# Last batch of the last expert layer: five places for the sorted tokens, two weight loads between the scatters, the residual behind the normalization

## What is computed

```python
def _moe_mlp(x, gate_w, gate_b, w1, w2):
    logits = xf @ gate_w + gate_b
    one_hot = jax.nn.one_hot(jnp.argmax(logits, axis=-1), E, dtype=xf.dtype)   # E = 8
    h = jax.nn.gelu(jnp.einsum('td,edh->teh', xf, w1), approximate=True)       # 128 -> 512
    y = jnp.einsum('teh,ehd->ted', h, w2)                                      # 512 -> 128
    return jnp.einsum('te,ted->td', one_hot, y)

x = x + _msa(_layernorm(x, ln1_w, ln1_b), w_qkv, w_proj)
x = x + _moe_mlp(_layernorm(x, ln2_w, ln2_b), gate_w, gate_b, w1, w2)
```

## Time and profile before

| | |
|---|---|
| median of 3 runs | 2741.87 us (2741.44 to 2743.07) |
| the profiled execution | 2746.61 us |
| its span, first to last instruction | 2744.8 us |
| mean granted TensorE clock | 0.951 of full |
| busy share of the span: TensorE, VectorE, ScalarE, GpSimd | 85%, 68%, 65%, 34% |

### The profile page before, as it was taken

One profiled execution on the slowest core, in us unless ns is written; L12 is line 12 of the kernel. 1 busy time (PEld: TensorE's weight loads), 2 busy tenths in 40 slices (PEclk: granted clock), 3 DMA queues, 4 the chain that ended last, 5 costly groups with the idle time before them and its releaser, 6 DMA issues. The chain is left out here.

```text
span 2744.8 us, 44545 instructions
## 1 busy us (share of the span) xinstructions
PE 2339.9 (85%) x15879; PEld 907.7 (33%) x15958; DVE 1856.2 (68%) x3041; ACT 1775.1 (65%) x3759; POOL 938.8 (34%) x1573
## 2 busy tenths in 40 slices
PE   5789889888888999888889989978989988989934
PEld 3222223222322344444444444312223323423414
DVE  6779897878787575454555655678986787687410
ACT  4278777767766655545556556568877777777721
POOL 5450132453264266337415133014023222213222
PEclk8699999999999999999999999999999999999967
DMA  4331113112313312431322222112013213202304
GB/s 157 118 119 28 32 31 112 42 58 84 105 28 94 97 52 66 134 94 41 113 77 65 64 61 65 39 55 67 23 32 109 88 30 115 88 20 68 98 27 159
DMA packets 151965, 202.80 MB, mean 74 GB/s; under 512 B 23472, under 2 KB 104240, under 8 KB 151568
## 3 DMA queue, kind: packets, MB, share of 16 engines
q1 hardware_dynamic: 133344, 138.83, 16.8%
q0 software_dynamic: 17536, 59.58, 6.9%
q10 hardware_dynamic: 864, 1.53, 0.2%
HBM read 138.40 MB, written 57.93 MB: 72 GB/s over the span
## 5 line engine op out<-in xcount | busy, mean ns | idle before, releaser
L1240 ACT ACTIVATE PB<-bank 128x512 f32<-128x512 f32 (+3 forms) x2944 | 1440.1, 557 | 592.4 <-PE bank L946 308.2
L1420 DVE TENSOR_REDUCE small<-unit 128x1 f32<-128x1024 f32 x1024 | 1211.1, 1218 | 245.3 <-PE unit L966 235.5
L966 PE MATMUL unit<-RK 61*128 61x512 bf16 (+4 forms) x2764 | 871.9, 375 | 144.9 <-DVE small L1420 87.4
L1086 PE MATMUL bank<-PB,VP 128*32 128x512 f32 (+3 forms) x5888 | 760.8, 569 | 14.6 <-ACT PB L1240 7.9
L946 PE MATMUL bank<-RK 64*128 64x512 bf16 x2048 | 677.9, 387 | 72.8 <-ACT PB L1240 38.4
L1417 DVE CUSTOM_DVE_ANT_0 unit<-unit,maskb 128x640 f32<-128x640 f32 (+7 forms) x512 | 387.8, 770 | 325.3 <-PE unit L966 306.3
L966 PEld LDWEIGHTS unit<-RK 61*128 61x128 bf16 (+1 forms) x2816 | 211.6, 95 | 579.9 <-issue 254.2
L946 PEld LDWEIGHTS bank<-RK 64*128 64x128 bf16 x2048 | 154.4, 94 | 504.8 <-ACT PB L1240 327.5
L1655 POOL CAST small<-small 128x8 bf16<-128x8 f32 x192 | 36.7, 191 | 764.1 <-DVE small L1420 557.2
L942 PE MATMUL bank<-RK 128*128 128x512 bf16 (+2 forms) x959 | 279.0, 300 | 2.4 <-ACT PB L1240 0.9
L941 PE MATMUL bank<-RK 128*128 128x256 bf16 (+3 forms) x934 | 268.9, 299 | 12.4 <-ACT PB L1240 4.5
(11 more groups left out here) (183 smaller groups left out, 2044.1 us busy)
## 6 DMA issues: line engine op xcount, KB each, us to landing
RK<-q_parts SPq DMA_DIRECT2D x128, 96.0 KB
RK<-k_parts SPq DMA_DIRECT2D x128, 96.0 KB
RK<-rq_parts SPq DMA_DIRECT2D x48, 192.0 KB
RK<-rk_parts SPq DMA_DIRECT2D x48, 192.0 KB
q_parts<-SC SPq DMA_DIRECT2D x32, 256.0 KB, 2.8
k_parts<-SC SPq DMA_DIRECT2D x32, 256.0 KB, 2.8
XSB<-x_sorted SPq DMA_DIRECT2D x40, 192.0 KB, 4.1
y_sorted<-XSB SPq DMA_DIRECT2D x40, 192.0 KB, 2.1
```

Source lines behind the costliest of these rows:

```text
L966: p = e.matmul(unit[k // 2 - 2][:, c0:c1], slot(L, u, 0, 0, rows)[:, 128 * qt:128 * qt + 128], slot(L, u, 1, 0, rows)[:, c0:c1], start=Tru ...
L1086: p = e.matmul(bank[k][32 * j:32 * j + 32, c0:512], VP[:, 8 * (pr // 8) + kt, 9 * h:9 * h + 32], prob(L, t)[:, c0:512], start=(kt == 0), s ...
L1240: e.activation(prob(L, t)[:, c0:512], bank[k][:, c0:512], ACT.Exp, scale=LAYERS[L].scale).then_inc(bank_free[k], 1)
L1420: e.tensor_reduce(m, unit[k // 2 - 2][:, :], AX.X, ALU.max, negate=True).then_inc(bank_free[k], 1)
```

## The change

Three things, all for the last batch of the last layer:

1. The five groups of sorted tokens have a place each: three in `XSB` and two in `PB`, the buffer of the attention's exponentials, which is no longer in use. All five `xload` are written behind the last scatter, and none behind a `ystore`.
2. The `wload` of tile 0 is issued behind the second scatter DMA and that of tile 1 behind the sixth; the other thirteen stay behind the last scatter.
3. `residual` also waits for VectorE's `ln_out`.

```diff
@@ def dispatch
         for i in range(4):
             yield t - 0.5
             P.do("scatter", M, b, i, total=P.count(("scatter", b), 32), after=t)
+            if (M, b) == (1, B - 1) and i % 2 == 0:
+                load_weights(M, b, i // 2, mo["tile"], t)
+
+    def load_weights(M, b, j, first, t):
+
+        k = j if (M, b) == (1, B - 1) and j >= WXN else (first + j) % WXN
+        return P.do("wload", M, b, j, slot=k, total=P.count(("wload", k), 16), after=t)
@@ def experts
-                k = (first // GROUP + q) % XS
+                k = (first // GROUP + q) % XS if q < XS or not last else q
@@
-                k = j if last and j >= WXN else (first + j) % WXN
-                here["w", j] = P.do("wload", M, b, j, slot=k, total=P.count(("wload", k), 16), after=t)
+                here["w", j] = P.end["wload", M, b, j] if last and j < 2 else load_weights(M, b, j, first, t)
@@
-                xload(j // GROUP + 2, t)
+                if not last:
+                    xload(j // GROUP + 2, t)
@@
-        xload(0, P.end["scatter", M, b, 3])
-        xload(1, P.end["scatter", M, b, 3])
+        for q in range(EGROUPS if last else 2):
+            xload(q, P.end["scatter", M, b, 3])
@@ def build
+        def tokens(k):
+
+            return XSB[:, k, :] if k < XS else PB[:, k - XS, 0:128 * GROUP]
@@ gpsimd, residual
+                    if b == B - 1:
+                        g.wait_ge(ln_done, ln_no["g1", b, 1])
                     e.tensor_tensor(xs, xs, zs, ALU.add).then_inc(residual, 1)
@@ sync, xload
-                    if s.n > XS:
+                    if s.n > XS and k < XS:
                         g.wait_ge(ystored[k], ystores[s.n - 1 - XS].more["total"])
```

More of the change, by code:

```diff
@@ L419, in collect @@
         for i in range(4):
-            t1 = P.do("collect", M, b, i, total=P.count(("collect", b), 32), stored=[P.total["ystore", k] for k in range(XS)],
+            t1 = P.do("collect", M, b, i, total=P.count(("collect", b), 32), stored=[P.total.get(("ystore", k), 0) for k in range(EGROUPS)],
                       after=t)
@@ L745, in build @@
         collected = [sem("collected%d" % b) for b in range(B)]
-        ystored = [sem("ystored%d" % k) for k in range(XS)]
-        xloaded = [sem("xloaded%d" % k) for k in range(XS)]
+        ystored = [sem("ystored%d" % k) for k in range(EGROUPS)]
+        xloaded = [sem("xloaded%d" % k) for k in range(EGROUPS)]
         wloaded = [sem("wloaded%d" % k) for k in range(ETILES)]
@@ L1128, in tensor @@
                     for j in range(GROUP):
-                        p = e.transpose(bank[k][:, 128 * j:128 * j + 128], XSB[:, x["slot"], 128 * j:128 * j + 128], identf[:, :])
+                        p = e.transpose(bank[k][:, 128 * j:128 * j + 128], tokens(x["slot"])[:, 128 * j:128 * j + 128], identf[:, :])
                     p.then_inc(bank_full[k], 1)
@@ L1536, in vector @@
                     x, w = step_of["xload", M, b, j // GROUP].more["slot"], step_of["wload", M, b, j]
-                    o = XSB[:, x, 128 * (j % GROUP):128 * (j % GROUP) + 128]
+                    o = tokens(x)[:, 128 * (j % GROUP):128 * (j % GROUP) + 128]
                     g.wait_ge(bank_full[k], n)
@@ L1697, in gpsimd @@
                     g.wait_ge(*tail)
-                    for k in range(XS):
+                    for k in range(EGROUPS):
                         g.wait_ge(ystored[k], s.more["stored"][k])
@@ L1743, in sync @@
                     g.wait_ge(scattered[b], 128 * (M + 1))
-                    if s.n > XS:
+                    if s.n > XS and k < XS:
                         g.wait_ge(ystored[k], ystores[s.n - 1 - XS].more["total"])
-                    e.dma_start(XSB[:, k, :].rearrange("p (j d) -> p j d", d=128),
+                    e.dma_start(tokens(k).rearrange("p (j d) -> p j d", d=128),
                                 XSD[b][r:r + 128 * GROUP, :].rearrange("(j p) d -> p j d", p=128)).then_inc(xloaded[k], 16)
@@ L1753, in sync @@
                     e.dma_start(YSD[b][r:r + 128 * GROUP, :].rearrange("(j p) d -> p j d", p=128),
-                                XSB[:, k, :].rearrange("p (j d) -> p j d", d=128)).then_inc(ystored[k], 16)
+                                tokens(k).rearrange("p (j d) -> p j d", d=128)).then_inc(ystored[k], 16)
                 elif kind == "fetch":
```

## The result

| | before | after |
|---|---|---|
| median of 20 runs each, first comparison | 2744.38 us (2740.11 to 2756.64) | 2735.49 us (2723.93 to 2744.16) |
| ratio, 95% interval | | 0.9963, 0.9951 to 0.9974 |
| median, second comparison (11 and 6 runs) | 2746.57 us | 2734.22 us |
| ratio, 95% interval | | 0.9950, 0.9936 to 0.9964 |
| span of the profiled execution | 2744.8 us | 2731.3 us |

The changed kernel is faster by 8.9 us of the medians in the first comparison, 12.4 in the second. The predicted time, 2729.6 us, missed the first median by 5.9 us and the range by 1.9 us. The sum of 12.3 us is 0.45% of the time; the interval of the ratio, 0.26% to 0.49%, holds it.

The account below looks back on a forecast made before the run. The prediction took the last batch's serial chain to bound the end: normalization, GpSimd's scatters, then TensorE waiting for late token loads. Terms of -2.13, +2.51, -13.04 and +0.4 us took 2741.9 to 2729.6 us; 8-in-10 range 2726.8 to 2733.6.

Parts of the forecast that it names:

- The sum of 12.3 us: Last batch to the end: all terms together, -2.13 + 2.51 - 13.04 + 0.4 = -12.3 us.
- The two large terms: Last batch: residual after the normalization, -2.13 us; all five token loads at once, no TensorE waits between groups, -13.04 us.
- the price of an issue: GpSimd's queue between scatters: 1.26 us per issue, so two weight loads delay the last scatter by 2.51 us.
- The clock term: First expert group on TensorE: the clock may rise later, 5.3 us instead of 3.4; half of +0.85 us taken, +0.4.
- Part 2: Two weight loads between the scatters: last scatter 2.51 us later, nothing given back on TensorE.
- slow scatter: Last scatter's landing: early weights in the shared DMA queue could delay it by up to +1.7 us; 0 taken.
- The upper bound: Second early weight load: 6.4 us to landing, so the last scatter could land 1.7 us later.
- My lower bound: Early weight load: through after some 3.7 us, before the last scatter would land anyway, so 0 cost.
- The slow opening: Rival, last batch: scatters wait for early weights, five loads crowd the first, +1.7 us each; 2733.0 us, chance 0.18.
- The third load waiting for the weights: Rival, token loads: the third lands only when the weight stream is through; sum -4.1, 2737.8 us, chance 0.07.
- The first load: Rival, token loads: the first waits for the weight stream; sum +5.4 us, 2747.3 us, chance 0.03.

Follow-up runs that it names:

- e1: Changed kernel without the two early weight loads, all fifteen behind the last scatter; ratio to the kernel before 0.9944.
- e2: Kernel before with only the residual's wait for the normalization; ratio to the kernel before 0.9978.
- e5: Kernel before with five token places, each later token load issued as late as before but ahead of the store; one run, 2749.60 us, before 2742.66.
- e9: Changed kernel without early weight loads, third to fifth token loads issued only once the third tile's weights landed; ratio to the kernel before 0.9965.
- e12: Changed kernel with 82 additional TensorE products ahead of the last batch's first token turning; ratio to the kernel before 0.9944.
- slowed comparison: Changed kernel and two versions with 64 additional products, compared with the kernel before; all runs took 2,804 to 2,829 us, ratios 0.9999, 0.9998 and 1.0002.
- e4: Kernel before with only the two early weight loads between the scatters; ratio to the kernel before 0.9996.
- e6: Kernel before with five token places, three token loads at once, the last two behind the stores of groups 0 and 1; one run, 2756.16 us, before 2742.66.
- e3: Kernel before with only the five places and five token loads at once; ratio to the kernel before 0.9945.
- e13: Changed kernel without early weight loads, third to fifth token loads behind the third tile's weights, 74 additional TensorE products; ratio to the kernel before 0.9965.
- e10: Changed kernel with 64 additional TensorE products ahead of the last batch's first token turning; ratio to the kernel before 0.9951.
- e11: Changed kernel without early weight loads, third to fifth token loads behind the third tile's weights, 64 additional TensorE products; ratio to the kernel before 0.9953.
- e7: Same kernel as e11, run in the slowed comparison; ratio to the kernel before 1.0002.

## Why the prediction was wrong in its number and right in its mechanism

**The sum.** -12.3 us were forecast, the stretch gave -12.29. By pieces of the chain, each measured in both kernels:

| piece | forecast | measured |
|---|---|---|
| start of the stretch to the list of tokens for the last scatter (`IX`): 24.86, then 22.75 us | -2.13 | -2.11 |
| to the last scatter's landing: 12.03, then 14.66 | +2.51 | +2.63 |
| to the first `up` product of group 1: 13.33, then 13.02 | +0.4 | -0.31 |
| to the first `up` product of group 4: 30.16, then 17.13 | -13.04 | -13.03 |
| to the end: 25.67, then 26.20 | 0 | +0.53 |

The two large terms and the price of an issue were right. That the sum is right to 0.01 us is luck: the third piece came out 0.7 us below its forecast and the fifth, where I had written that the collect is as before, 0.5 above it. The clock term was also badly founded. I set 3.4 us, counted from the first `up` product, beside 5.3, counted from the first turning; counted alike they are 5.1 and 5.3 from the turning, 3.4 and 4.4 from the products. That the rise could come later was true all the same, as e1, e2, e5 and e9 show (5.0 to 5.7 us after the products began). In the changed kernel it came at 2.9; e12 shows that 1.4 us hang on it in the products and 0.35 in the turning.

**The step that failed** is the one behind the sum: "these terms don't depend on it, so I take them off the median", and in the range "half a microsecond of scatter of the runs". The median of three runs, 2741.87, was not the kernel's: 20 runs give 2744.38, 2.5 us more. And the scatter is not half a microsecond: the changed kernel's 20 runs go from 2723.93 to 2744.16, with a standard deviation of 4.9 us; that of the kernel before is 4.4. It was there to be seen, since the profiled execution stood 4.7 us above the three. Of the 5.9 us by which I missed, 2.5 are the base; the other 3.4 are about what two medians of 20 such runs can differ by (some 1.8 us as a standard deviation, estimated from the 4.4 and 4.9), and the second comparison gave -12.4 of the medians. That they are scatter and nothing else is not shown. A range for this kernel needed some 3 us on either side for that alone.

**Where the scatter comes from.** Over the 20 runs the time and the mean granted clock go together (correlation -0.94, worked out from the list of runs): the slowest, 2744.16, had 0.949, the fastest, 2723.93, had 0.958. The starts of the stretch, ahead of which no instruction differs, lie, outside the slowed comparison, between 2629.37 (e4, clock 0.956) and 2655.03 us (e6, 0.943). That the clock causes it is the reading nearest to hand; no run here set the clock ahead of the last batch.

**Part 2.** I wrote "the two loads give nothing back on TensorE". Where TensorE starts at the low clock that was nearly right: without them e1 waited 0.23 us for weights and e3 not at all, and the first tokens came 0.2 to 0.3 us later. With a warm TensorE it is wrong by 0.8 us (e13). The cost in time was not additive: alone (e4) it was +0.3, since the third load of tokens landed with the stream's end, which came 2.4 us sooner. The 1.7 us of a slow scatter did not occur: it landed in 2.23 us. The upper bound had the weight load under way for 6.4 us, and the early ones landed in 4.2. My lower bound, 3.7, was too short: the 440 KB that I gave to the one weight load held a load of tokens and part of the next weights too. The Trainium skill's page "DMA: Bandwidth & Descriptors", section "Queues, rings and completion order", by which the scatter's signal comes behind every earlier write, would give 4.2 us less the 2.56 us between the issues, 1.6 us, which is less than the 2.23 that the scatter takes anyway; no run here tells that rule from none.

**Rivals.** The slow opening did not happen (3.94 us). The third load waiting for the weights is half true: a load issued 16 us or more behind the last scatter does (e4, e5, e6 and the kernel before), one issued after 10 us comes late for a warm TensorE but long before the stream's end (e13), one issued at once holds nothing up. I had named the question rightly, and it was settled by the time of issue. The rule of turns among queues of the same page and section of the Trainium skill, which speaks against that rival, was not tested by itself. Against the stream's end as the only gate it has e13's load, which got through some 8 us before it; but that load took 8.46 us where one with idle engines took 2.6, and the rule alone gives no figure for that. The first load never waited.

## What to carry to other kernels

A short load that is wanted soon belongs ahead of a long stream of large ones: issued with the stream's start it landed here in 3.9 to 4.3 us, 10 us into it in 8.5, and when issued 16 us into it in 7.3 to 11.0, with the stream's end. A place ahead of the store in its own queue won under 1 us. A cost found in one version (two issues ahead of the last scatter) need not be the cost in another: it vanished where a wait for the stream's end stood behind it. When one version comes out less good than its parts say, read the clock in both before a wait is blamed: e1 has a wait for weights on its chain, and most of its loss was the clock. A sum that fits to a hundredth can hold two errors of half a microsecond. Before a forecast of a few microseconds is given as a time, look at how far single runs lie apart; three runs that agree don't show it.

## What the runs showed of the hardware

The residual and VectorE's first instruction were recorded as starting 0.04 us apart, VectorE's first, and still VectorE's took 2465 ns, the length of GpSimd's. TensorE's granted clock rose 2.9, 3.4, 5.0, 5.2 and 5.7 us after the same `up` products began in five profiles (the changed kernel, before, e1, e9, e5), and in e11 it was low again when the tokens came, 2.5 us after TensorE had fallen idle. Warming it up for 16 us was worth nothing in e10 and e11, where it ended that much too early. It is not a sure thing either way: in e7, of the slowed comparison, the profile has TensorE idle for 2.78 us and the first turning still at the high clock, 0.55 us. GpSimd issued scatters and weight loads alike at 1.26 us each, and a weight load of 524 KB landed in 4.2 us as one of the first three of the changed kernel, in 6.3 to 6.4 as one of the first three with two loads of tokens beside them and none early (before, e9), and in 6.8 to 8.2 with five loads of tokens (e1).
